# Two PSUM banks shared by the output product and the transposed combination, and another order of set-up, in a fused attention and feed-forward kernel

## What is computed

```python
sa, ca, ga, sb, cb, gb = rows of (silu(c) @ wmod)
ga = (2*(ga >= 0) - 1) * maximum(abs(ga), 0.25)         # gb likewise
h = layernorm(x) * (1 + ca) + sa
q = heads(h @ Wq.T); sigma_q = elu(q) + 1                # 16 heads of 32
a = einsum(sigma_q, memories) / clip(einsum(sigma_q, memory_norms), EPS)   # 4 banks n
a = a * active                                           # bank switched off if its norms sum to < EPS
combined = einsum(a, softmax(bank_weights))              # sum over the 4 banks
x = x + ga * (combined @ Wo.T)
h = layernorm(x) * (1 + cb) + sb
hid = silu(h @ w_gate) * (h @ w_up)                      # 2048 wide
x = x + gb * (keep_largest_2_of_4(hid) @ w_down)
```

## Time and profile before

| | |
|---|---|
| median of 3 runs | 1412.52 us (1411.31 to 1418.31) |
| profiled execution | 1408.14 us, span 1406.3 us |
| mean granted clock of TensorE | 0.995 of 2.4 GHz |
| set-up and tile 0 | 0 to 83.3 us |
| tiles 1 to 6 | 38.36 us each |
| tile 7 and the change to phase B | about 313 to 380 us |

### The profile page before, as it was taken

How to read it: one execution, slowest core, us unless ns; L and a number is a source line. 1 busy time by engine, 2 the same in 40 slices (tenths; PEclk the granted TensorE clock), 3 DMA queues, 4 the chain that set the end, 5 groups by cost and what they waited for, 6 DMA issues and landing times.

```text
span 1406.3 us, 18635 instructions
## 1 busy us (share of the span) xinstructions
PE 1360.8 (97%) x6838; PEld 1115.1 (79%) x6838; DVE 869.0 (62%) x1243; ACT 511.0 (36%) x805; POOL 561.7 (40%) x395
## 2 busy tenths in 40 slices
PE   7799999997999999999999999999999999999998
PEld 5677777776778888888888888788888888888887
DVE  6787777768684545555554656575555555563646
ACT  5466676765632222212222234331212212222211
POOL 1766666665171313133232345571313223232312
PEclk9899999999999999999999999999999999999999
DMA  6302212223320201101020302230201101020102
GB/s 248 121 33 118 89 60 89 90 85 143 132 97 0 98 30 67 61 36 67 30 90 7 127 30 97 91 127 1 97 34 63 67 30 67 30 97 0 67 0 97
DMA packets 24126, 102.43 MB, mean 73 GB/s; under 512 B 2688, under 2 KB 3232, under 8 KB 14496
## 3 DMA queue, kind: packets, MB, share of 16 engines
q1 hardware_dynamic: 24096, 102.05, 19.4%
HBM read 68.47 MB, written 33.57 MB: 73 GB/s over the span
## 4 chain that ended last, share of the span: by engine, by line
PE 78%; DVE 13%; ACT 4%; issue 3%; POOL 1%; DMA 1%; SPq 0%; DVEq 0%; ACTq 0%
PE bank L1168 25%; PE bank L1170 25%; PE bank L1169 25%; DVE banks_r L984 4%; DVE inv_norm L972 1%; PE bank L1192 1%; DVE ln_raw L811 1%; ACT up_w_hi L682 1%; DVE x_ring L947 1%; PE bank L1246 1%; DVE h_abs L1113 1%; POOL up_w_lo L458 1%; DVE bank L942 1%; ACT xn L518 1%; DMA x_ring<-in_x_dram 1%
## 5 line engine op out<-in xcount | busy, mean ns | idle before, releaser
L1072 DVE TENSOR_TENSOR h_act<-bank,silu_g 128x512 f32<-128x512 f32 x128 | 88.1, 690 | 403.4 <-PE bank L1170 382.2
L464 POOL TENSOR_TENSOR hs_lo<-h_abs,hs_hi 128x512 fp32r<-128x512 f32 x124 | 169.9, 1400 | 378.6 <-ACT hs_hi L704 378.6
L414 POOL TENSOR_TENSOR h_lo<-h_raw,h_hi 128x512 fp32r<-128x512 f32 x64 | 124.7, 1976 | 233.0 <-ACT h_hi L687 233.0
L1168 PE MATMUL bank<-h_hi,up_w_hi 128*128 128x512 f32 x512 | 199.8, 390 | 3.8 <-DVE up_w_lo L960 1.7
L1168 PE MATMUL bank<-h_hi,gate_w_hi 128*128 128x512 f32 x512 | 199.7, 390 | 0.6 <-ACT silu_g L719 0.5
L1170 PE MATMUL bank<-h_hi,gate_w_lo 128*128 128x512 f32 x512 | 199.2, 389 | 0.0
L1169 PE MATMUL bank<-h_lo,up_w_hi 128*128 128x512 f32 x512 | 199.2, 389 | 0.0
L1170 PE MATMUL bank<-h_hi,up_w_lo 128*128 128x512 f32 x512 | 199.2, 389 | 0.0
L1169 PE MATMUL bank<-h_lo,gate_w_hi 128*128 128x512 f32 x512 | 199.2, 389 | 0.0
L719 ACT ACTIVATE silu_g<-bank 128x512 f32<-128x512 f32 x128 | 75.9, 595 | 329.3 <-PE bank L1170 329.2
L704 ACT ACTIVATE hs_hi<-h_abs 128x512 fp32r<-128x512 f32 x124 | 72.7, 628 | 331.8 <-DVE h_abs L1113 209.0
(11 more groups left out here) (145 smaller groups left out, 2379.5 us busy)
## 6 DMA issues: line engine op xcount, KB each, us to landing
h_raw<-h2T_scratch SPq DMA_DIRECT2D x16, 1024.0 KB, 4.8
x_ring<-in_x_dram SPq DMA_DIRECT2D x8, 1024.0 KB, 4.8
x_scratch<-x_ring SPq DMA_DIRECT2D x8, 1024.0 KB, 3.9
h2T_scratch<-h_full SPq DMA_DIRECT2D x8, 1024.0 KB, 3.8
over_x<-x_scratch SPq DMA_DIRECT2D x8, 1024.0 KB, 4.8
acc_scratch<-over_x SPq DMA_DIRECT2D x8, 1024.0 KB, 3.9
over_x<-acc_scratch SPq DMA_DIRECT2D x8, 1024.0 KB, 4.8
out_dram<-over_x SPq DMA_DIRECT2D x7, 1024.0 KB, 3.9
```

Of the source, the lines that this page charges most:

```text
L414: nc.gpsimd.tensor_tensor(h2_lo[:, k], h2_raw[:, k], h2_hi[:, k].bitcast(F32), ALU.subtract).then_inc(h2_lo_done, 1)
L464: nc.gpsimd.tensor_tensor(hs_lo[:, j], h_abs[:, j], hs_hi[:, j].bitcast(F32), ALU.subtract).then_inc(hs_lo_done, 1)
L1072: nc.vector.tensor_tensor(h_act[:, cc, j], bank[2 * (j % 2) + 1][:], silu_g[:, j % 2], ALU.mult).then_inc(h_done, 1)
L1168: nc.tensor.matmul(out_, stat[0], mov[0], start=start, stop=False)
```

## The change

Subtile u now uses bank 4 + u % 2 for both its transposes and its product: the product overwrites the transposed combination once both halves have been read. `comb_transpose` waits for `x1_done` of subtile u-2, which used the same bank, where it waited for `combT_lo` of subtile u-1; `wo_product` no longer waits for `x1_done`. The output weights' low half is made on GpSimd in four instructions. On VectorE, `gate_cols` takes 2 instructions for 8 and `mem_bd` 4 for 16; the statistics of x tile 1 move out of tile 0 into the set-up, two subtiles before `sigma_of(0, 2)` and two, with aggregation and variance, before the gates.

```diff
@@ GpSimd
-            nc.gpsimd.tensor_tensor(wo_lo[:], h2_full[:], wo_hi[:].bitcast(F32), ALU.subtract).then_inc(wa_lo, 1)
+            for g in range(K):
+                ins = nc.gpsimd.tensor_tensor(wo_lo[:, g], h2_full[:, g], wo_hi[:, g].bitcast(F32), ALU.subtract)
+            ins.then_inc(wa_lo, 1)
@@ ScalarE, combT_high
-                nc.scalar.activation(combT_hi[par][:].rearrange("p k n -> p (k n)"), bank[5][:],
+                nc.scalar.activation(combT_hi[par][:].rearrange("p k n -> p (k n)"), bank[4 + par][:],
                                      ACT.Copy).then_inc(combT_hi_done, 1)
@@ VectorE, set-up
-            for pair in range(PAIR * K):
-                ins = nc.vector.tensor_tensor(gate_cols[:, pair],
-                                              bank_sb[:, PAIR * pair:PAIR * (pair + 1)].rearrange("p h n -> p n h"),
-                                              active_sum[:].unsqueeze(2).broadcast_to([P, NB, PAIR]), ALU.mult)
+            by_head = gate_cols.rearrange("p b n h -> p b h n")
+            for h in range(PAIR):
+                ins = nc.vector.tensor_tensor(by_head[:, :, h], bank_sb[:, h::PAIR],
+                                              active_sum[:].unsqueeze(1).broadcast_to([P, PAIR * K, NB]), ALU.mult)
             link(ins)
             sigma_of(0, 0)
-            for k in range(K):
-                for hh in range(HG):
-                    rows = slice(DH * hh, DH * hh + DH)
-                    pair, h = hh // PAIR, hh % PAIR
-                    ins = nc.vector.tensor_tensor(mem_bd[rows, k, :, h, :], mem_raw[rows, k],
-                                                  gated(rows, PAIR * k + pair, h), ALU.mult)
+            for hh in range(HG):
+                rows = slice(DH * hh, DH * hh + DH)
+                pair, h = hh // PAIR, hh % PAIR
+                gated = gate_cols[rows, pair::PAIR, :, h].unsqueeze(3).broadcast_to([DH, K, NB, DH])
+                ins = nc.vector.tensor_tensor(mem_bd[rows, :, :, h, :], mem_raw[rows], gated, ALU.mult)
             ins.then_inc(mem_bd_ready, 1)
             sigma_of(0, 1)
+            dve.wait_ge(x_in[place(1)], 16)
+            for s in (0, 1):
+                ln_stats(1, 0, s, bn1_done)
             sigma_of(0, 2)
...
+            for s in (2, 3):
+                ln_stats(1, 0, s, bn1_done)
+            dve.wait_ge(bn1_done, 8)
+            ln_aggregate(1, 0, ag1_done)
+            ln_variance(0)
             dve.wait_ge(gate_sign_done, 2)
             dve.wait_ge(gate_abs_done, 2)
@@ VectorE, attn_rest
-                nc.vector.tensor_tensor(bank[4][:], bank[4][:], ga_all[:, b], ALU.mult
+                o = bank[4 + sp_ % 2]
+                nc.vector.tensor_tensor(o[:], o[:], ga_all[:, b], ALU.mult
@@ VectorE, tile, if first
                     scale_banks(u, 0, first)
-                    x_wait()
-                    stats(0, 1, 2, 3)
-                    dve.wait_ge(bn1_done, 8)
-                    ln_aggregate(t + 1, 0, ag1_done)
-                    ln_variance(0)
@@ TensorE
-            def comb_transpose(u, first=False):
+            def comb_transpose(u, par, first=False):
                 pe.wait_ge(comb_done, u + 1)
                 if not first:
-                    pe.wait_ge(combT_lo_done, u)
+                    pe.wait_ge(x1_done, u - 1)
                 for g in range(K):
-                    ins = nc.tensor.transpose(bank[5][:, g * P:(g + 1) * P], combined[:, g], ident[:])
+                    ins = nc.tensor.transpose(bank[4 + par][:, g * P:(g + 1) * P], combined[:, g], ident[:])
                 ins.then_inc(combT_done, 1)
 
-            def wo_product(u, par, first=False, blocks=range(K)):
+            def wo_product(u, par, blocks=range(K)):
                 if blocks[0] == 0:
                     pe.wait_ge(combT_lo_done, u + 1)
-                    if not first:
-                        pe.wait_ge(x1_done, u)
                 for g in blocks:
-                    ins = mm3(bank[4][:], (combT_hi[par][:, g], combT_lo[par][:, g]),
+                    ins = mm3(bank[4 + par][:], (combT_hi[par][:, g], combT_lo[par][:, g]),
                               (wo_hi[:, g], wo_lo[:, g]), g == 0, g == K - 1)
```

More of the change, by code:

```diff
@@ L882, in _ @@
                 "p (b n h) -> p b n h", n=NB, h=PAIR)
-            def gated(rows, blk, h):
-                return gate_cols[rows, blk, :, h].unsqueeze(2).broadcast_to([DH, NB, DH])
             for hh in range(HG):
@@ L946, in attn_rest @@
                 xs = x_ring[:, place(tp), sp_]
-                nc.vector.tensor_tensor(xs, bank[4][:], xs, ALU.add).then_inc(x1_done, 1)
+                nc.vector.tensor_tensor(xs, o[:], xs, ALU.add).then_inc(x1_done, 1)
                 if stats:
@@ L952, in combT_low @@
                 dve.wait_ge(combT_hi_done, u + 1)
-                nc.vector.tensor_tensor(combT_lo[par][:].rearrange("p k n -> p (k n)"), bank[5][:],
+                nc.vector.tensor_tensor(combT_lo[par][:].rearrange("p k n -> p (k n)"), bank[4 + par][:],
                                         combT_hi[par][:].rearrange("p k n -> p (k n)").bitcast(F32),
@@ L1320, in tile @@
                     pe.wait_ge(gates_ready, 1)
-                comb_transpose(u, first=first)
+                comb_transpose(u, 0, first=first)
                 banks_of(t, 2)
@@ L1326, in tile @@
                     pe.wait_ge(wa_lo, 1)
-                wo_product(u, 0, first=first, blocks=(0, 1))
+                wo_product(u, 0, blocks=(0, 1))
                 if not last:
@@ L1331, in tile @@
                 wo_product(u, 0, blocks=(2, 3))
-                comb_transpose(u + 1)
+                comb_transpose(u + 1, 1, first=first)
                 banks_of(t, 3)
@@ L1347, in tile @@
                     t2(t - 1, 1)
-                comb_transpose(u + 2)
+                comb_transpose(u + 2, 0)
                 if last:
@@ L1364, in tile @@
                         if g == 2:
-                            comb_transpose(u + 3)
+                            comb_transpose(u + 3, 1)
             def gate_or_up(t2, cc, chunk, j, m, first=False):
@@ L1422, in _ @@
             wo_product(4 * NT - 2, 0)
-            comb_transpose(4 * NT - 1)
+            comb_transpose(4 * NT - 1, 1)
             gate_or_up(0, 0, 0, 0, 1, first=True)
```

## The result

The changed kernel takes 1397.45 us (1396.58 to 1397.53, four runs), the one before 1412.16 us beside it (1411.31 to 1418.31, four runs): a ratio of 0.989 [0.986, 0.991]. The forecast was 1402.0 with 1395 to 1409; the profiled execution was expected at 1397.6 and took 1396.58, with a span of 1394.7 us against 1406.3.

A forecast was written before the change was run, and what follows sets the result against it. The prediction took TensorE's 45.5 us of idle time as all that could be won; 6.9 us from set-up and tile 0 plus 3.6 from six looped tiles made 10.5, from a median of 1412.52 to 1402.0 us, range 1395 to 1409.

The forecast's parts named there:

- What bounds it, and the steady tiles: Looped tiles 1 to 6: VectorE's gapless chain limits the gain to 0.60 us a tile, not 1.69; 3.6 us together.
- the forecast's 0.8: Middle tile: TensorE's wait before the second product stays about 0.8 us (0.78), because VectorE's chain has not moved.
- The last tile's zero: Last tile: no gain taken; what the product gains is given back at the transpose waiting for GpSimd's combination.
- The added wait: Transposes of subtile u waiting for x of subtile u-2: 3.3 us to spare at the tightest, so costed at nothing.
- What was called covered in the set-up: Possible next late items: first transposed combination's low half ready at 50.4, wanted at 51.5; gates and rows near 48.
- Set-up: Banks of subtile 2 start at about 47.7 instead of 54.11: 6.4 us, or 6.9 with tile 0's wait.
- Rival 2: Set-up: line 931 loses every border and waits for all four pieces, to 42.8; 8.2 us gained, 1404.3; chance 0.14.
- TensorE's clock: Banks of subtile 2: a high clock could gain up to 1.2 us more, kept for the range, not the sum.
- The sum and the median: 6.9 + 3.6 = 10.5 us: span 1395.8, profiled execution 1397.6; as that ran 4.4 us below the median, median 1402.0.

The follow-up runs named there:

- e1: Changed kernel with the set-up of the kernel before, so the shared banks alone: 1404.52 us, ratio 0.995.
- e2: Kernel before with the new set-up, products in bank 4 and transposes in bank 5 as before: 1405.41 us, ratio 0.994.
- e10: Changed kernel with twelve extra products, results never read, ahead of the last tile's banks 3: 1397.92 us, ratio 0.987.
- e4: Changed kernel with the output weights' low half in one GpSimd instruction again: 1400.68 us.
- e5: Changed kernel with the statistics of the second x tile back in tile 0, behind the first scaled banks: 1399.05 us.
- e9: e8 plus the output weights' low half in one GpSimd instruction, the gates' sign in PSUM and e10's extra products: 1395.35 us, ratio 0.987.
- e11: e8 with `ln_shift` made by four one-element VectorE instructions whose second factor is a scalar operand: 1396.61 us, ratio 0.989.
- e6: Changed kernel with 8 and 16 small VectorE products again instead of 2 and 4: 1397.92 us.
- e8: Changed kernel without VectorE's epsilon instruction (line 821); ScalarE's square root adds the epsilon as a bias: 1395.75 us, ratio 0.987.
- e3: Kernel before with only the output weights' low half split into four GpSimd instructions: span 1407.7 us.
- e7: Kernel before, long GpSimd instruction kept, with line 931 in two halves that read the gates' sign from PSUM: span 1408.4 us.

## Why the prediction was right

**What bounds it, and the steady tiles.** Borne out. The releaser went from line 947 to `combT_lo`, and a tile won 0.64 us for the 0.60 forecast, not the 1.69 of its waits. The reason given, a chain on VectorE without a gap, is seen in the waits that are left. They are 0.22 and 0.50 us, where 0.3 and 0.8 were written. The waits fell by 1.69 - 0.72 = 0.97 us and the tile by 0.64: the rest is PE's busy time, 36.98 us in e1's tile 4 with shared banks and 36.67 in e2's tile 5 without, for the same instructions (a few records can be missing). Most of it is a wait that is too short to be listed as one. Between the two halves of the banks of subtile 3 PE goes on without a pause in the kernel before:

```profile
138.91 0.28 PE L1246 MATMUL bank<-mem_lo,sigma_hi 64*128 64x256 f32 x2
139.03 0.28 PE L1246 MATMUL bank<-mem_hi,sigma_hi 64*128 64x256 f32 x2
```

After, the same two starts are 129.16 and 129.41, and the next follows at 129.64 (139.15 in the kernel before): 0.48 us for 0.24. The second half waits for the scaled banks of subtile 2 (`banks_r_done` in `banks_of`), and VectorE's line 991 ends at 126.89 + 2.47 = 129.36. PE comes earlier and VectorE's chain hasn't moved, just as with the second product. 0.50 + 0.24 us are the forecast's 0.8, nearly. The last tile's zero was off by 0.45 us in this execution, to the other side, and the forecast had no term for it: the low clock under a whole product (e10). Other executions lose nothing there.

**The added wait.** Costed at nothing, and no row of the waits shows it. The transposes at 127.93 run without idle time. What was called covered in the set-up was covered too, but by little: the low half of the first transposed combination is ready at 49.20 + 0.69 = 49.89, and PE's first product starts at 50.06, where 50.4 and 51.5 were written.

**Set-up.** The banks of subtile 2 were to start at 47.7 and start at 47.59. Inside the sum there are errors that cancel: the merged products took 2.76 us, not 2.5; the pieces 5.17, not 5.04; line 937 got the first border and ended at 39.47, not the second and 40.6. That the last made no difference was stated: GpSimd's chain sets the end. The pieces run from 37.89 to 43.06, the half-sums and the combination to 46.88, and PE's transposes start at 47.03. Rival 2, that the next piece always wins at a border, fell in the set-up. In the tiles, e1 and e2 show that it isn't wrong everywhere: there the next piece does win at times. And an arrival behind a border waits for the rest of the piece: `ln_shift` in tile 0 of the changed kernel begins at 44.43, behind the border at 43.03 + 2.50/2 = 44.28, and takes 1.12 us.

**TensorE's clock.** The 1.2 us that were kept for the range came: the banks of subtile 2 ran at 2.4 GHz. Whether they come differs between executions, so that they came in the profiled one is luck, and it was right to leave them out of the sum: in e2, e4, e5, e9 and e11 the same stretch ran at about 1.2 GHz, in e6, e8 and e10 at 2.4.

**The sum and the median.** 10.5 us forecast for the span, 11.6 measured: the clock's 1.24, less 0.45 in the last tile and 0.2 in the second part, and 0.2 in the tiles and 0.3 in the set-up and tile 0 on top. Without the clock's luck it would be 10.4. For the median, I had carried over the 4.4 us by which before's profiled execution lay below the median of the runs shown. This is the step that failed: the changed kernel's profiled execution lies 0.9 us below its median. The forecast was 4.5 us too high, inside its range: 3.5 by this offset, the rest by the span. The range's lower end, 1395, isn't the sum that is given for it, either: 1402.0 - 1.2 - 4.4 = 1396.4.

**Where that offset comes from.** The likely cause is in good part the toss on `ln_shift`. Before's profiled execution had no lost one, no low clock in the loop, and none in the last tile, where e3 and e7 had it. In the profiled executions with bank 4 and bank 5 as before (before, e2, e3, e7), 8 of 24 looped tiles have it, at 1.1 to 2.8 us each, so 2 a run and 2 to 5 us. With shared banks (after, e1, e4, e5, e6, e10) it is 1 of 36. The ordinary executions of before leave no trace, so that they lose tiles this way isn't shown; what they do show is mean clocks of 0.984 to 0.993 beside the experiments, where before's profiled one had 0.995. That is more than lost tosses account for (0.96 over one tile of 41 us is 0.001 of the whole), so other stretches at the low clock must belong to it, such as the set-up: the first 40 us have 0.83 in e1 and e2 and 0.96 in before. Why the shared banks make the loss rarer stays open: VectorE reaches the border 0.04 us ahead of it in the changed kernel and 0.05 in the kernel before (138.57, with GpSimd's border at 137.34 + 1.28), no difference that these traces can resolve. In the 60 tiles together the nine held arrivals come 0.02 to 0.04 us ahead of the border, the others 0.035 to 0.055.

## What to carry to other kernels

Before you add up the waits that a change removes, look at the queue of the engine that ends them: if it runs without a gap, only the step by which the released instruction moves ahead in that queue is won, here 0.60 of 1.69 us. Look for VectorE instructions that are too long for their size; if they end with a GpSimd instruction, cut that into pieces or move one operand to PSUM. And don't carry the distance between one profiled execution and the median from one kernel to the next: it is made of events, lost tosses and stretches at the low clock, that differ from one execution to the next, and that the change may make rarer.

## What was new about the hardware

- **A border is a toss.** VectorE's four-element instruction reached the border of two back-to-back GpSimd instructions 0.02 to 0.055 us ahead of it (the border taken as the middle of the two). Mostly it was let in (0.17 us); nine times in the 60 looped tiles counted above it was held for the whole second one (1.31 to 1.33 us), and a tile lost 1.1 or 2.7 us. The held ones were those that came closest, 0.02 to 0.04 us ahead; between 0.035 and 0.04 both happened. In the set-up line 937 (933 in e3) came 1.0 us ahead of a border, in the changed kernel and in e3, waited for it and was let in both times.
- **What is held.** Beside a GpSimd instruction that reads SBUF: two SBUF operands were (4.55 us for 256 elements, 0.97 us for 4), and line 821 with one operand of 4 elements (1.07 us), for a reason that no run tested. Not held were a second operand in PSUM (e7) and one-element instructions with a scalar operand (e11, 0.58 us for four).
- **The clock behind short idle times.** The banks of subtile 2 ran at 2.4 GHz behind an idle time of 1.29 us (after) and of 2.85 us (e6, window at 1.00), but at 1.2 GHz behind 0.63 us (e11) and 2.03 us (e9). The length of that idle time alone doesn't tell which; it is worth 1.2 us. The Trainium skill, TensorE: Matmul & The Clock Gate, "Part 1: The HAM clock gate (the "warmup" mystery)", calls the number of products that run cold run-variable. These runs agree: the same products took 1.62 us in the changed kernel and 2.86 in e11.
- **Merging.** Sixteen VectorE products of 128 elements on 32 partitions took 5.73 us (e6), four of 512 elements 2.76. One of the sixteen took 1.28 us, by all signs held beside GpSimd's line 401, and their median is 0.28 us, so that unheld they would take 4.5 us by estimate. On GpSimd, 2048 elements in one instruction took 4.55 us and in four 5.17.
